# Second attention: two gathered rows per unit over 32 units in place of four over 16, and the first queries normalised ahead of the first gathers

## The chip, the core and the metric

The kernel runs on one core of a Trainium2 chip. The metric is the device time of one execution in microseconds, lower is better. The core has five engines with their own instruction queues, each worked off in order: PE (TensorE, matrix products), DVE (VectorE), ACT (ScalarE), POOL (GpSimd) and SP (SyncE, which only starts transfers here). They wait for one another through semaphores.

## What is computed

`x` is (8, 256, 256) in float32. Two blocks follow each other, and each does `x = x + attention(norm(x)) * silu(ffn(norm(x)))`. The change lies in the second block:

```
q, k, v = heads of xn @ wq.T, xn @ wk.T, xn @ wv.T     # 16 heads of 128
q = rope(rmsnorm(q, q_norm_w));  k = rope(rmsnorm(k, k_norm_w))
scores = 50 * tanh(q @ k.T * 128**-0.5 / 50), causal
s = softmax(scores) @ v @ wo.T
weights, indices = top_k(sigmoid(xn @ gate_w.T) + gate_b, 4)
g = shared_ffn(xn) + sum over the token's four experts of weight * expert(xn)
x = x + s * silu(g)
```

## The kernel before, in words

After the first block come the feed-forward part of the second block (a shared network, then 79 tiles of 128 routed rows), and then the second attention, from about 700 us to the end. The experts' results lie in DRAM, one row for each token and each of its four experts. They must be fetched back and added, weighted, to the gate sum `g1`. That is done beside the second attention.

The second attention is 64 units: 8 pairs of heads times 8 sequences of 256 tokens. A unit `n` goes through a pipeline that is three units deep, and each engine has the order of its work written out in a function `unit_pair(w, first)` of 16 units, run four times:

- PE in unit `n`: products for queries and keys in two halves (`project_qk`), transposes of the keys and of the normalised queries of unit `n-1` (`transposes_qk`), the product for the values (`project_v`), the mix with the values of `n-2` (`mix1`), the output product of `n-3` (`project_o`), the scores of `n-1` (`scores1`, lines 811 to 818; its first product, L817, marks the beat of a unit below), and the transposes of the mixed heads of `n-2` (`transposes_y`).
- ACT: copies `xs` (queries and keys) and `v` out of the accumulators, copies the transposed queries, takes tanh of the scores, rounds the transposed heads of `n-2` to `yT1h`, takes the exponential. In units 3 to 6 of every eight it also rounds a quarter of the next weights (`unit_hi`).
- DVE in unit `n`: squares and their sums in two halves (L1603, L1605), the mean squares (L1610), the scaled transposed keys `kT` of `n-1` (L1615), the division of the heads of `n-2`, the sum over heads of `n-3`, the low part `yT1l` of the heads of `n-2` (`out_lo`, L1212), and then, in the first 16 units, `combine(i)`: four operations (L1633), each adding one gathered row times its weight to `g1`, for the 128 tokens of tile `i`. In units 3 to 6 of every eight it ends with the low part of a quarter of the next weights (`unit_lo`, L1212, tile `bw_l`).
- POOL in unit `n`: `norm_q(n)` (a power, L1799, and two products, L1802), the causal mask of unit `n-1` (`mask`, L1811), and in the first 15 units `fetch_rows(i+1)`: four indirect gathers (L1827) of 128 rows each. Before unit 0 it waits until all rows of the experts are stored and issues `fetch_rows(0)`.

So tile `v` of 16 takes four gathers in one unit of POOL and four additions in one unit of DVE, one unit later than the gathers. `yg` has two buffers of four rows; a gather into a buffer waits until the tile before the last has been added (semaphore `g1_sb`). `gate_out1` (L1640) and `gate_tanh_out` turn `g1` into the gate in units 48 to 55.

Of the kernel before, what the change touches and what calls it, by code (L numbers as in the profile page):

```python
# [30 lines left out]
P = 128  # L31
NB, T, D = 8, 256, 256
TT, KD = T // P, D // P
NT = NB * TT
# [9 lines left out]
NE, TOPK, HE = 16, 4, 176  # L44
EW = KD * 2 * HE + 2 * D
NS = NT
CELLS = (NE + 1) * NT
NTILE = TOPK * NT + NE - 1
GROUP = 8
# [6 lines left out]
def build(nc, x, pack_qk, pack_vo, pack_w1, pack_w3, pack_w2, pack_attn, pack_experts, pack_shared, gate_b, q_norm, k_norm,  # L56
          rope_cosT, rope_sinT, ident_c, hadamard_c, tri_add_c, tri_mul_c, q_row_c, k_rows_c, before_c, route_c, out):
    ctx = ExitStack()
    with ctx:
        def sem(name):  # L60
            return ctx.enter_context(nc.semaphore(name))
# [22 lines left out]
        def region(start, end):  # L84
# [145 lines left out]
        y2_stored = [sem(f"y2_stored{j}") for j in range(GROUP)]  # L230
        xg_ps, up2_ps, z2_ps, down2_ps = (sem(n) for n in ("xg_ps", "up2_ps", "z2_ps", "down2_ps"))
        xT_sb, h2_sb, u2_sb, th2_sb, z2_sb, zT_sb, y2_sb, z2_clear = (sem(n) for n in (
            "xT_sb", "h2_sb", "u2_sb", "th2_sb", "z2_sb", "zT_sb", "y2_sb", "z2_clear"))
        yg_loaded = [sem("yg_loaded0"), sem("yg_loaded1")]
        g1_sb, thg_sb, gate_sb, so_sb, o_sb_made = (sem(n) for n in (
            "g1_sb", "thg_sb", "gate_sb", "so_sb", "o_sb_made"))

# [2 lines left out]
        def after(eng, s, value):  # L240

            if isinstance(value, int) and value <= 0:
                return
            eng.wait_ge(s, value)
# [956 lines left out]
        def _(dve):  # L1201
# [293 lines left out]
            def unit_lo(v, par, q):  # L1495
                half = (A_LOADS + par) % 2
                dve.wait_ge(bw_hi, 4 * v + q + 1)
                c = slice(512 * q, 512 * q + 512)
                lo(bw[par][1][:, c], raw[:, half, c], bw[par][0][:, c]).then_inc(bw_lo, 1)
# [100 lines left out]
            def squares(n, i, tt):  # L1600
                dve.wait_ge(xs_sb, 2 * n + tt + 1)
                x_qk = xs[:, i % 2, tt, :, :, :].rearrange("p s h e -> p (s h e)")
                dve.tensor_tensor(out=sq[:, tt, :], in0=x_qk, in1=x_qk, op=ALU.mult).then_inc(sq_sb, 1)  # L1603
                dve.wait_ge(sq_sb, 2 * n + tt + 1)
                dve.tensor_reduce(out=ssq[:, i % 2, tt, :], in_=sq[:, tt, :].rearrange("p (h e) -> p h e", h=4),  # L1605
                                  axis=AX.X, op=ALU.add).then_inc(ssq_sb, 1)

            def mean_squares(n, i):
                dve.wait_ge(ssq_sb, 2 * n + 2)
                dve.tensor_scalar(out=msq[:, i % 2, :], in0=ssq[:, i % 2, :, :].rearrange("p t h -> p (t h)"),  # L1610
                                  scalar1=1.0 / E1, scalar2=RMS_EPS, op0=ALU.mult, op1=ALU.add).then_inc(msq_sb, 1)

            def key_T(n, i, unit):
                dve.wait_ge(kT1_ps, n + 1)
                dve.tensor_tensor(out=kT1[:, i % 2, :, :], in0=more[:, 2, :].rearrange("p (h t) -> p h t", h=2),  # L1615
                                  in1=qk_scale[:, bass.ds(2 * unit, 2)].unsqueeze(2).to_broadcast([P, 2, T]),
                                  op=ALU.mult).then_inc(kT1_sb, 1)

            def heads_out1(n, i):
                dve.wait_ge(y1_ps, n + 1)  # L1620
                o = more[:, 0:2, 0:2 * (E1 + 1)].rearrange("p t (h e) -> p t h e", h=2)
                dve.reciprocal(out=rden1[:, i % 2, :, :], in_=o[:, :, :, E1]).then_inc(rden1_sb, 1)
                dve.wait_ge(rden1_sb, n + 1)
                dve.tensor_tensor(out=y1[:, i % 2, :, :, :], in0=o[:, :, :, 0:E1],
                                  in1=rden1[:, i % 2, :, :].unsqueeze(3).to_broadcast([P, TT, 2, E1]), op=ALU.mult)\
                   .then_inc(y1_sb, 1)

            def combine(v):

                dve.wait_ge(yg_loaded[v % 2], 16 * TOPK * (v // 2 + 1))  # L1630
                for k in range(TOPK):
                    after(dve, g1_sb, TOPK * v + k)
                    dve.scalar_tensor_tensor(out=g1[:, v, :], in0=yg[:, v % 2, k, :], scalar=prob_all[:, v, k:k + 1],  # L1633
                                             in1=g1[:, v, :], op0=ALU.mult, op1=ALU.add).then_inc(g1_sb, 1)

            def gate_out1(b):

                dve.wait_ge(thg_sb, b + 1)
                g = g1[:, TT * b:TT * b + TT, :].rearrange("p t d -> p (t d)")
                dve.scalar_tensor_tensor(out=g, in0=th_g[:], scalar=1.0, in1=g, op0=ALU.add, op1=ALU.mult)\  # L1640
                   .then_inc(gate_sb, 1)
# [11 lines left out]
            def add_unit(n, i, first, last=False):  # L1653
                b = i % NB
                dve.wait_ge(o1_ps, n + 1)
                s = s_acc[:, 2 * b:2 * b + 2, :].rearrange("p t d -> p (t d)")
                if first and 0 <= i < NB:
                    dve.tensor_copy(s, banks[1][:, :]).then_inc(acc1, 1)
                else:
                    after(dve, acc1, n + 1 - NB)  # L1660
                    dve.tensor_tensor(out=s, in0=banks[1][:, :], in1=s, op=ALU.add).then_inc(acc1, 1)
                if last:
                    block_out(b, s)

            def out_lo(n, i):
                dve.wait_ge(yT1h_sb, n + 1)
                lo(yT1l[:, i % 2, :, :].rearrange("p h t -> p (h t)"), trio[:, 2, :],
                   yT1h[:, i % 2, :, :].rearrange("p h t -> p (h t)")).then_inc(yT1l_sb, 1)

            def unit_pair(w, first, final):  # L1670
                for i in range(2 * NB):
                    n = 2 * NB * w + i

                    def live(lag):
                        return not first or i >= lag
                    squares(n, i, 0)
                    squares(n, i, 1)
                    mean_squares(n, i)
                    if live(1):
                        key_T(n - 1, i - 1, 2 * w + (i - 1) // NB)  # L1680
                    if live(2):
                        heads_out1(n - 2, i - 2)
                    if live(3):
                        add_unit(n - 3, i - 3, first, final and i - 3 >= NB)
                    if live(2):
                        out_lo(n - 2, i - 2)
                    if first:
                        combine(i)
                    if final and i < NB:
                        gate_out1(i)  # L1690
                    if 3 <= i % NB < 7 and not (final and i >= NB):
                        unit_lo(2 * w + i // NB + 1, (i // NB + 1) % 2, i % NB - 3)

            dve.wait_ge(rope_made, 6)
            unit_pair(0, True, False)
            for w in range(1, NU // 2 - 1):
                unit_pair(w, False, False)
            unit_pair(NU // 2 - 1, False, True)
            n = NU * NB
# [11 lines left out]
        def _(pool):  # L1711
# [84 lines left out]
            def norm_q(n, i):  # L1796
                r = i % 2
                pool.wait_ge(msq_sb, n + 1)
                pool.tensor_tensor(out=rstd[:, r, :], in0=msq[:, r, :], in1=half_pow[:], op=ALU.pow).then_inc(rstd_sb, 1)  # L1799
                pool.wait_ge(rstd_sb, n + 1)  # L1800
                for tt in range(TT):
                    last = pool.tensor_tensor(out=qn[:, r, tt, :, :], in0=xs[:, r, tt, 0, :, :],  # L1802
                                              in1=rstd[:, r, 4 * tt:4 * tt + 2].unsqueeze(2).to_broadcast([P, 2, E1]),
                                              op=ALU.mult)
                last.then_inc(qn_sb, 1)
# [8 lines left out]
            def unit_pair(w, first):  # L1814
                for i in range(2 * NB):
                    n = 2 * NB * w + i
                    norm_q(n, i)
                    if not first or i >= 1:
                        mask(n - 1, i - 1)
                    if first and i < NT - 1:  # L1820
                        fetch_rows(i + 1)

            def fetch_rows(v):

                after(pool, g1_sb, TOPK * (v - 1))
                for k in range(TOPK):
                    pool.indirect_dma_start(  # L1827
                        out=yg[:, v % 2, k, :], out_offset=None, in_=rows_dram,
                        in_offset=bass.IndirectOffsetOnAxis(ap=slots_all[:, v, k:k + 1], axis=0),
                        bounds_check=CELLS * P - 1, oob_is_err=False).then_inc(yg_loaded[v % 2], 16)  # L1830

            pool.wait_ge(down2_ps, NS + NTILE)
            pool.memset(v1[:].rearrange("p r t h e -> p (r t h) e")[:, :, E1:E1 + 1], 1.0).then_inc(v1_ones, 1)
            for j in range(GROUP):
                pool.wait_ge(y2_stored[j], 16 * ((NTILE - 1 - j) // GROUP + 1))
            fetch_rows(0)
            unit_pair(0, True)
            for w in range(1, NU // 2):
                unit_pair(w, False)
# [95 lines left out]
```

## Time and profile before

| | |
|---|---|
| median of 3 runs | 1366.03 us (1360.82 to 1368.21) |
| the profiled execution, own time | 1364.2 us |
| its span, first to last instruction | 1362.4 us |
| busy: PE, DVE, ACT, POOL | 1257.5, 847.7, 596.2, 472.7 us |
| mean granted PE clock | 0.975 of full speed |
| gathers (L1827) | 64, 68.7 us on POOL |
| additions (L1633) | 64, median 485 ns, longest 1391 ns |

Views are of this one execution. In a row of a timeline stand the start in us from the beginning of the span, the time in us, the engine, the source line, the operation, the tiles written and read, the shape, a count (x4 are four such instructions in a row), and in brackets the idle time of the engine before it with what ended it. Matrix products overlap, so a busy PE is a modelled one. The view by stretches gives for each window its length, the busy time of each engine with a count of instructions, the granted clock of PE (1.00 is 2.4 GHz) and the share and rate of transfers.

### The profile page before, as it was taken

The page shows a single profiled execution, that of the slowest core. Times are in us where ns is not written, and L with a number is a line of the kernel's source. Part 1 is how long each engine was busy: PE and PEld are TensorE (multiplying, and loading weights), DVE is VectorE, ACT ScalarE, POOL GpSimd, SP SyncE. Part 2 cuts the span into 40 slices and gives each one's busy share as a digit, 9 for nine tenths or more (in the row PEclk, how much of TensorE's full clock was granted, in tenths as well). Part 3 has the DMA queues.
Part 4 walks back from the last instruction along what each step waited for, and adds up shares of the span by engine and source line. Part 5 has one row for each costly group of instructions (what it writes and reads, how often), then busy time and mean ns, then how long its engine had stood idle before and what let it go on. Part 6 is the DMA issues. An engine that isn't in the chain of part 4 may idle for free.

```text
span 1362.4 us, 25374 instructions
## 1 busy us (share of the span) xinstructions
PE 1257.5 (92%) x9326; PEld 1095.7 (80%) x9326; DVE 847.7 (62%) x1733; ACT 596.2 (44%) x1351; POOL 472.7 (35%) x488
## 2 busy tenths in 40 slices
PE   5699989999988879999988899999999999999996
PEld 4588878778777757777767888899999999998995
DVE  4647567557556654434447777776666767676785
ACT  3333323323323335555544444445454545555552
POOL 0112332332431220000028787644434344434442
PEclk9799999989999989999999999999999999999998
DMA  5754224234100953333331221100000000000000
GB/s 203 280 194 152 104 103 151 78 129 148 47 33 27 346 188 105 105 103 103 109 121 53 67 65 47 63 1 32 1 1 32 1 32 1 1 1 1 1 32 32
DMA packets 63674, 112.20 MB, mean 82 GB/s; under 512 B 6977, under 2 KB 36033, under 8 KB 62017
## 3 DMA queue, kind: packets, MB, share of 16 engines
q1 hardware_dynamic: 57408, 93.79, 19.6%
q0 software_dynamic: 6144, 16.79, 3.7%
q8 instruction: 78, 1.28, 0.4%
q14 instruction: 44, 0.35, 0.1%
HBM read 49.86 MB, written 60.69 MB: 81 GB/s over the span
## 4 chain that ended last, share of the span: by engine, by line
PE 82%; DVE 8%; issue 4%; ACT 3%; another core or an unknown queue 2%; DMA 1%; POOL 0%; SPq 0%; ACTq 0%; DVEq 0%; POOLq 0%
PE bank L703 7%; PE six L720 6%; PE six L817 5%; PE bank L779 4%; PE bank L781 4%; PE bank L780 4%; PE bank L390 4%; PE bank L391 3%; PE bank L392 3%; PE bank L854 2%; PE bank L853 2%; PE bank L852 2%; PE bank L791 2%; PE six L831 2%; PE bank L792 2%
## 5 line engine op out<-in xcount | busy, mean ns | idle before, releaser
L1799 POOL TENSOR_TENSOR rstd<-msq,half_pow 128x8 f32<-128x8 f32 x64 | 105.4, 1647 | 156.6 <-DVE msq L1610 156.2
L1128 ACT ACTIVATE pT<-six,rstd 128x256 f32<-128x256 f32 x128 | 60.7, 475 | 215.3 <-PE six L818 212.9
L1736 POOL TENSOR_TENSOR hid_l<-hid,hid_h 128x256 fp32r<-128x256 f32 x64 | 48.0, 750 | 241.2 <-ACT hid_h L950 241.2
L1811 POOL TENSOR_TENSOR pT<-pT,tri_mul 128x512 f32<-128x512 f32 x64 | 84.3, 1316 | 129.1 <-ACT pT L1174 129.1
L1212 DVE TENSOR_TENSOR yT1l<-six,yT1h 128x512 fp32r<-128x512 f32 x64 | 44.3, 692 | 135.5 <-ACT yT1h L1179 135.5
L1603 DVE TENSOR_TENSOR sq<-xs 128x512 f32<-128x512 f32 x128 | 104.2, 814 | 17.2 <-ACT xs L1147 17.2
L703 PE MATMUL bank<-experts,xT 128*128 x316 | 109.5, 469 | 0.8 <-ACT xT L1072 0.8
L779 PE MATMUL bank<-bw_h,xT1h 128*128 128x512 f32 x256 | 106.2, 415 | 0.7 <-issue 0.7
L781 PE MATMUL bank<-bw_l,xT1h 128*128 128x512 f32 x256 | 100.5, 392 | 0.0
L780 PE MATMUL bank<-bw_h,xT1l 128*128 128x512 f32 x256 | 100.1, 391 | 0.0
L817 PE MATMUL six<-qT,kT 128*128 128x256 f32 x256 | 79.3, 392 | 19.0 <-issue 15.6
L1605 DVE TENSOR_REDUCE ssq<-sq 128x4 f32<-128x512 f32 x128 | 87.8, 686 | 4.4
L1152 ACT ACTIVATE v<-bank 128x512 f32<-128x512 f32 x64 | 38.3, 598 | 102.5 <-PE bank L793 102.5
L720 PE MATMUL six<-experts,zT 128*128 x316 | 81.5, 380 | 1.2 <-DVE zT L1552 1.2
L852 PE MATMUL bank<-bw_h,yT1h 128*128 128x256 f32 x256 | 77.4, 302 | 3.8 <-DVE yT1l L1212 3.8
L390 PE MATMUL bank<-xT0h,w_h 128*128 128x256 f32 x256 | 77.9, 304 | 2.7 <-DVE w_l L1212 2.5
L1802 POOL TENSOR_TENSOR qn<-xs,rstd 128x256 f32<-128x256 f32 x128 | 78.4, 632 | 5.1
L1147 ACT ACTIVATE xs<-bank 128x512 f32<-128x512 f32 x128 | 74.5, 618 | 8.2 <-PE bank L781 4.8
L791 PE MATMUL bank<-bw_h,xT1h 128*128 128x256 f32 x256 | 77.5, 303 | 0.5
L1552 DVE COPY zT<-six 128x256 f32<-128x256 f32 x95 | 40.3, 424 | 58.8 <-PE six L711 53.8
L929 ACT ACTIVATE pT<-six 128x768 f32<-128x768 f32 x64 | 48.4, 808 | 63.9 <-PE six L447 42.3
L1827 POOL DMA_INDIRECT yg<-cells_scratch,slots_all x64 | 68.7, 1074 | 20.1 <-issue 20.1
(282 smaller groups left out, 3926.7 us busy)
## 6 DMA issues: line engine op xcount, KB each, us to landing
cells_scratch<-zeros SPq DMA_DIRECT2D x8, 4352.0 KB, 14.8
xg<-cells_scratch SPq DMA_DIRECT2D x79, 128.0 KB, 2.0
cells_scratch<-y SPq DMA_DIRECT2D x79, 128.0 KB, 1.7
experts<-pack_experts_dram SPq DMA_DIRECT2D x16, 608.0 KB
raw<-pack_attn_dram SPq DMA_DIRECT2D x8, 1024.0 KB
raw<-pack_w_dram SPq DMA_DIRECT2D x2, 1024.0 KB
xT_scratch<-xT1h_c SPq DMA_DIRECT2D x8, 256.0 KB, 2.1
xT_scratch<-xT1l_c SPq DMA_DIRECT2D x8, 256.0 KB, 2.7
```

The lines of the kernel that those rows point to most:

```text
L390: pe.matmul(o, wh, mh, start=first, stop=False)
L703: last = pe.matmul(banks[j % 2][:, 0:2 * HE], xT[:, j % 2, k, :], weights(e, k * 2 * HE, 2 * HE), start=k == 0, stop=k == KD - 1)
L720: last = pe.matmul(six[:, 4 + r, 0:D], zT[:, r, c, :], w, start=c == 0, stop=c == 1)
L779: pe.matmul(banks[tt][:, :], xT1h[:, k, c], w[0][:, k, :], start=k == 0, stop=False)
L780: pe.matmul(banks[tt][:, :], xT1l[:, k, c], w[0][:, k, :], start=False, stop=False)
L781: last = pe.matmul(banks[tt][:, :], xT1h[:, k, c], w[1][:, k, :], start=False, stop=k == KD - 1)
L791: pe.matmul(o[:, tt, :], xT1h[:, k, c], w[0][:, k, :], start=k == 0, stop=False)
L817: pe.matmul(s_b[:, 0, h * T:(h + 1) * T], kT1[:, r, h, 0:P], qT1[:, r, h, :], start=True, stop=True)
L852: pe.matmul(o[:, tt, :], yT1h[:, r, h, c], w[0][:, h, :], start=h == 0, stop=False)
L1603: dve.tensor_tensor(out=sq[:, tt, :], in0=x_qk, in1=x_qk, op=ALU.mult).then_inc(sq_sb, 1)
L1605: dve.tensor_reduce(out=ssq[:, i % 2, tt, :], in_=sq[:, tt, :].rearrange("p (h e) -> p h e", h=4), axis=AX.X, op=ALU.add).then_inc(ssq_sb, 1)
L1799: pool.tensor_tensor(out=rstd[:, r, :], in0=msq[:, r, :], in1=half_pow[:], op=ALU.pow).then_inc(rstd_sb, 1)
```

## The change

Gathers and additions go by half tiles. `fetch_rows(u)` issues the gathers of two rows of tile `u // 2`, and `combine(u)` adds two. POOL issues `fetch_rows(n)` in unit `n` after the mask, for `n` from 0 to 31, and DVE runs `combine(n-1)` at its old place in the order of a unit, for `n` from 1 to 32. Four semaphores stand in for two. The wait for the stored rows of the experts, and the first gathers, come after `norm_q(0)` instead of before it, and DVE has no `combine` in unit 0 any more. The number of gathers and of additions stays 64 each.

```diff
-        yg_loaded = [sem("yg_loaded0"), sem("yg_loaded1")]
+        yg_loaded = [sem(f"yg_loaded{n}") for n in range(4)]
...
-            def combine(v):
-
-                dve.wait_ge(yg_loaded[v % 2], 16 * TOPK * (v // 2 + 1))
-                for k in range(TOPK):
+            def combine(u):
+
+                v, ks = u // 2, range(u % 2 * 2, u % 2 * 2 + 2)
+                dve.wait_ge(yg_loaded[u % 4], 32 * (u // 4 + 1))
+                for k in ks:
                     after(dve, g1_sb, TOPK * v + k)
                     dve.scalar_tensor_tensor(out=g1[:, v, :], in0=yg[:, v % 2, k, :], scalar=prob_all[:, v, k:k + 1],
                                              in1=g1[:, v, :], op0=ALU.mult, op1=ALU.add).then_inc(g1_sb, 1)
...
-                    if first:
-                        combine(i)
+                    if 1 <= n <= 2 * NT:
+                        combine(n - 1)
...
                     norm_q(n, i)
                     if not first or i >= 1:
                         mask(n - 1, i - 1)
-                    if first and i < NT - 1:
-                        fetch_rows(i + 1)
-
-            def fetch_rows(v):
-
+                    if n == 0:
+                        for j in range(GROUP):
+                            pool.wait_ge(y2_stored[j], 16 * ((NTILE - 1 - j) // GROUP + 1))
+                    if n < 2 * NT:
+                        fetch_rows(n)
+
+            def fetch_rows(u):
+
+                v = u // 2
                 after(pool, g1_sb, TOPK * (v - 1))
-                for k in range(TOPK):
+                for k in range(u % 2 * 2, u % 2 * 2 + 2):
                     pool.indirect_dma_start(
                         out=yg[:, v % 2, k, :], out_offset=None, in_=rows_dram,
                         in_offset=bass.IndirectOffsetOnAxis(ap=slots_all[:, v, k:k + 1], axis=0),
-                        bounds_check=CELLS * P - 1, oob_is_err=False).then_inc(yg_loaded[v % 2], 16)
+                        bounds_check=CELLS * P - 1, oob_is_err=False).then_inc(yg_loaded[u % 4], 16)
 
             pool.wait_ge(down2_ps, NS + NTILE)
             pool.memset(v1[:].rearrange("p r t h e -> p (r t h) e")[:, :, E1:E1 + 1], 1.0).then_inc(v1_ones, 1)
-            for j in range(GROUP):
-                pool.wait_ge(y2_stored[j], 16 * ((NTILE - 1 - j) // GROUP + 1))
-            fetch_rows(0)
             unit_pair(0, True)
```

## Rows read from the trace of the kernel before

**Rows 1.** Busy time by stretches: start of the attention, first 16 units, later units
```profile
700.60:720.00 19.40, 12.47 (x65) 10.47 (x64) 9.20 (x16) 4.46 (x8) 13.74 (x15) 0.94 0.49 172
...
840.00:870.00 30.00, 26.07 (x187) 23.93 (x186) 24.97 (x44) 13.47 (x28) 23.17 (x22) 1.00 0.22 66
...
940.00:980.00 40.00, 40.00 (x281) 37.08 (x280) 25.89 (x42) 21.09 (x47) 16.68 (x17) 1.00 0.08 28
```

**Rows 2.** Timeline of PE, first 16 units: the first score products of five units
```profile
738.50 0.67 PE L817 MATMUL six<-qT,kT 128*128 128x256 f32 x2 [0.86 <-issue]
...
771.95 0.67 PE L817 MATMUL six<-qT,kT 128*128 128x256 f32 x2 [1.31 <-issue]
...
783.10 0.67 PE L817 MATMUL six<-qT,kT 128*128 128x256 f32 x2 [1.32 <-issue]
...
793.65 0.67 PE L817 MATMUL six<-qT,kT 128*128 128x256 f32 x2 [0.72 <-issue]
...
880.43 0.67 PE L817 MATMUL six<-qT,kT 128*128 128x256 f32 x2 [0.73 <-issue]
```

**Rows 3.** Timeline of DVE, two of the first 16 units
```profile
778.87 0.69 DVE L1212 TENSOR_TENSOR bw_l<-raw,bw_h 128x512 fp32r<-128x512 f32 x1
...
786.56 0.69 DVE L1212 TENSOR_TENSOR yT1l<-six,yT1h 128x512 fp32r<-128x512 f32 x1 [2.15 <-ACT yT1h L1179]
787.17 2.94 DVE L1633 SCALAR_TENSOR_TENSOR g<-yg,prob_all,g 128x256 f32<-128x256 f32 x4
790.02 0.68 DVE L1603 TENSOR_TENSOR sq<-xs 128x512 f32<-128x512 f32 x1
...
792.86 0.68 DVE L1615 TENSOR_TENSOR kT<-six,qk_scale 128x512 f32<-128x512 f32 x1
```

**Rows 4.** Instructions of line L1633 in one unit, ns shortest/median/longest
```profile
L1633 DVE SCALAR_TENSOR_TENSOR g<-yg,prob_all,g x2: 486/934/1383, 787.7 to 789.1; 128x256 f32<-128x256 f32 x2
```

**Rows 5.** Timeline of POOL in the same unit: the mask and the first gather
```profile
787.34 1.45 POOL L1811 TENSOR_TENSOR pT<-pT,tri_mul 128x512 f32<-128x512 f32 x1 [1.33 <-ACT pT L1174]
788.94 1.09 POOL L1827 DMA_INDIRECT yg<-cells_scratch,slots_all  x1 [0.16 <-issue]
```

**Rows 6.** Timeline of PE, later units: the first score products of five units
```profile
890.11 0.59 PE L817 MATMUL six<-qT,kT 128*128 128x256 f32 x2
...
909.23 0.59 PE L817 MATMUL six<-qT,kT 128*128 128x256 f32 x2
...
1196.88 0.62 PE L817 MATMUL six<-qT,kT 128*128 128x256 f32 x2
...
1226.27 0.67 PE L817 MATMUL six<-qT,kT 128*128 128x256 f32 x2
...
1236.48 0.67 PE L817 MATMUL six<-qT,kT 128*128 128x256 f32 x2
```

**Rows 7.** Timeline of DVE in a later unit, which has no addition
```profile
904.27 1.38 DVE L1603 TENSOR_TENSOR sq<-xs 128x512 f32<-128x512 f32 x1 [0.53 <-ACT xs L1147]
...
907.80 0.68 DVE L1615 TENSOR_TENSOR kT<-six,qk_scale 128x512 f32<-128x512 f32 x1
```

**Rows 8.** Timeline of PE at the start of the attention
```profile
712.17 0.66 PE L808 MATMUL six<-ident,qn 128*128 128x128 f32 x4 [2.91 <-POOL qn L1802]
...
717.55 1.20 PE L817 MATMUL six<-qT,kT 128*128 128x256 f32 x2 [3.29 <-DVE kT L1615]
```

**Rows 9.** Timeline of DVE at the start of the attention
```profile
706.17 0.34 DVE L1610 TENSOR_SCALAR msq<-ssq 128x8 f32<-128x8 f32 x1
711.76 2.20 DVE L1633 SCALAR_TENSOR_TENSOR g<-yg,prob_all,g 128x256 f32<-128x256 f32 x4 [5.25 <-DMA yg<-cells_scratch,slots_all]
```

**Rows 10.** Timeline of POOL at the start of the attention
```profile
709.18 1.68 POOL L1799 TENSOR_TENSOR rstd<-msq,half_pow 128x8 f32<-128x8 f32 x1
```

**Rows 11.** Timeline of ACT at the start of the attention
```profile
714.79 0.59 ACT L1168 ACTIVATE qT<-six 128x512 f32<-128x512 f32 x1
```

**Rows 12.** Chain of waits at the start of the attention: start, us, what
```profile
708.15 3.58 DMA yg<-cells_scratch,slots_all
```

## Prediction

> **What bounds the kernel now.** I first looked at the page's forty slices. PE is busy nearly everywhere, but its digits fall to 8 in the five slices in which POOL's rise to 7 and 8: the first 16 of the 64 attention units. The view by stretches gives the size [rows 1]: in 30 us of the first 16 units PE is busy 26.07 us and POOL 23.17, in 40 us of later units PE is busy 40.00 of 40.00. POOL looks like the culprit, so I went to the timelines of the engines to see who waits for whom.
>
> The beat is the first score product of a unit on PE. In the first 16 units it comes at 771.95, 783.10 and 793.65, so 11.15 and 10.55 us apart, with PE idle 1.32 and 0.72 us just before it [rows 2]. From the third of these products at 738.50 to the sixteenth at 880.43 there are 13 intervals in 141.93 us: eight of 11.15 and five of 10.55 make 141.95. In the later units 32 intervals take 1196.88 - 890.11 = 306.77 us, 9.59 each [rows 6]. That is PE's own work, and the floor.
>
> What holds PE back is DVE's order. From the score product at 783.10: DVE finishes its `yT1l` (started 786.56) and starts the four additions at 787.17; the squares of the next unit start at 790.02, the keys at 792.86 (0.68 long), and at 793.65 PE multiplies with them [rows 2, 3]. The loop closes there, 10.55 us long. The unit before has `bw_l` between the additions and the squares (778.87), which makes the 11.15. The additions sit in this loop with 790.02 - 787.17 = 2.85 us. POOL is not in it: it stood idle 1.33 us before its mask [rows 5], waiting for ACT, which waited for the scores.
>
> The four additions aren't equal. The second is the long one, 1383 ns against 486 for the one after it [rows 4], and it lies beside the mask on POOL (787.34 to 788.79 [rows 5]). In a later unit, without additions, the same stall falls on the squares: 1.38 us instead of 0.68 [rows 7, 3]. So the stall of about 0.9 us belongs to the mask, and stays.
>
> **First 16 units: additions from four to two.** What goes is the third and the fourth, 2 x 0.486 = 0.97 us [rows 4]; counted from the end of the stalled one (787.68 + 1.38 = 789.06) to the squares at 790.02 it is 0.96, and DVE starts an independent operation up to 0.09 us before the last one ends. I take 1.0 us. Bounds: 0.96 from these rows, and 1.43 (half of the 2.85) if the stall shrank too. The eight intervals with `bw_l` then go from 11.15 to 10.15, still DVE's: 8 x 1.0 = 8.0 us. The five others would go to 9.55, just below PE's floor of 9.59: 5 x 0.96 = 4.8 us. Late next in these is PE itself.
>
> The Trainium skill (SBUF — State Buffer, "Who interferes with whom") says that a VectorE operation with two inputs in SBUF and a GpSimd operation that reads SBUF can't run together, and the later one waits for the whole of the other. The trace agrees with it in the 1383 ns; by this rule the stall stays and the price is two times 0.486, without it one would halve the whole block.
>
> **Units 16 to 31: two additions more.** In the loop of a later unit the keys start at 907.80, end at 908.48, and PE needs them at 909.23 [rows 6, 7]: 0.75 us of slack, and DVE was idle 0.53 us before the squares. Two additions of 0.97 fit, nearly to the hundredth (9.55 against 9.59), in the eight units without weights: cost 0, and 0.3 us in all at most if it misses by 0.04. With `bw_l` the loop is 10.15 against 9.59: 0.56 x 8 = 4.5 us lost. The trace has a precedent: 1226.27 to 1236.48 is 10.21 us [rows 6], a unit in which DVE has one other operation more (`gate_out1`) beside `bw_l`. With 10.21 the loss is 5.0, and the bound from above is that the eight others lose as much, 10.0 in all.
>
> **Gathers, two per unit over 32 units.** In the first 16 they take some 2.8 us off POOL, which bounds nothing there: worth 0 beyond the start. In units 16 to 31 they come after the mask. There POOL is busy 16.68 of 40 us, 4.0 in a unit of 9.59 [rows 1]; two gathers at about 1.4 from start to start (an estimate: the first of a group is 1.09 long [rows 5], and a gap follows) bring it to 6.8. The mask begins 4.24 us and ends 5.69 us after the score product [rows 2, 5], the gathers are issued by 8.5, and the next power waits for DVE's mean squares, which come just ahead of the keys, 8.8 us after the product with two additions (792.86 - 1.0 - 783.10). So they hide in POOL's wait for DVE. Without that cover each us beyond would delay the normalised queries by one, and PE's transposes wait for those.
>
> The new semaphores and the `g1_sb` wait of a gather add nothing: a buffer is reused four units later, after the additions of two units before.
>
> **The start.** DVE has the mean squares of unit 0 at 706.17 + 0.34 = 706.51 [rows 9], but POOL issues the first four gathers first and starts the power at 709.18 [rows 10]; PE waits 2.91 us for the queries until 712.17 [rows 8]. Then DVE, in `combine(0)`, waits 5.25 us for the gathers and adds until 713.96, and only then squares unit 1, so PE waits another 3.29 us for keys until 717.55 [rows 8, 9]. The stores that POOL waited for before the gathers are long done when `norm_q(0)` is, so moving it past them costs nothing; what now comes after it, two gathers, runs beside PE's value product, and the power of unit 1 follows them.
>
> After the change the queries are ready 709.18 - 706.51 = 2.67 us earlier, PE does the same transposes and value product, and ACT's copy of the transposed queries (714.79 + 0.59 = 715.38 [rows 11]) moves to 712.7. DVE loses the wait of 5.25 us, so the keys, ready at about 717.4 before, are ready by 712.2; their input is there, since PE made it before it stood still at 712.17 - 2.91 = 709.26. First score product: about 712.8 instead of 717.55, 4.75 us earlier. Bounds: 2.67 if only POOL's delay goes, 6.2 if both of PE's waits (2.91 + 3.29) go.
>
> The next two intervals, 717.55 to 738.50, take 20.95 us. The first product pair there lasts 1.20 us, later 0.67 [rows 8, 2], and the granted clock of the stretch is 0.94 [rows 1]: PE had stood still for 3.29 us and fell to 1.2 GHz. With at most 1.3 us of standing, as in the units of 11.15 whose clock is 1.00, it should not fall. I put 8.9 for the first (10.2 less 1.3) and 9.6 for the second: 2.4 us gained. Bounds: 1.0 (two additions once, the clock falls as before) and 3.8.
>
> **The sum.** 8.0 + 4.8 + 4.75 + 2.4 - 4.5 = 15.45 us. The profiled execution took 1364.2 us, so 1348.8; it lies 1.8 us under the median of 1366.03, from which the same sum gives 1350.6. I take 1350.
>
> **Rivals.**
>
> *A: the block halves.* If the stall shares in it, the loop loses 1.43 us: intervals of 9.72 and 9.59, gains of 8 x 1.43 + 4.8 = 16.2 and a loss of 8 x 0.13 = 1.0. Sum 22.4, 1342 to 1344. The same time would come out if POOL were the bound. For it: POOL's digits in the slices. Against it: POOL's idle 1.33 us [rows 5], and squares that stall without any addition [rows 7].
>
> *B: the second 16 units give more back, or the start gives less.* If all sixteen units there lose 0.62 (10.21 less 9.59), 10.0 us are paid, and the sum is 10; if instead the start gives only 2.67 + 1.0, it is 12. Both together 4.7. Time 1354 to 1361. For it: the slack in the units without weights is 0.04 us by my count.
>
> *C: the loop doesn't shorten,* because something that I don't see is late just behind DVE, and 16 more units get the longer one. Only the start remains, 1359 to 1366.
>
> *D, slower: DVE waits for rows that have not landed.* The last gather of a group took 3.58 us from issue to landing [rows 12], and DVE waited at the start [rows 9]. Now there are 32 such waits, in front of squares on which PE depends. The last of two gathers is issued 7.2 us after a score product (788.94 - 783.10, and 1.4 for the next) and needed 9.59 + 4.07 = 13.7 us after it: 6.4 us of slack. From a landing time of 6.4 us on, each unit pays the excess; the gain is used up when the excess is 15.4 / 32 = 0.5 us, and a landing of 7.3 us would give 1364 + 13 = 1377. Against it: no DVE wait for rows is seen inside the units above, with a slack of only about 4.5 us.
>
> **Chances.** My forecast 0.68, with its own range 1345 to 1355; A 0.08; B 0.15; C 0.06; D 0.03. I count 0.5%, 6.8 us, as what a measurement of this kernel can tell from no change. Faster by more than that: the forecast, A and most of B, 0.89. Within 0.5%: the rest of B and C, 0.08. Slower: D, 0.03. The range that should hold the time 8 times in 10 reaches over A's edge and half of B: 1342 to 1357.
>
> **What would show it.** The interval of score products: about 10.15 with `bw_l` and 9.6 without, in the first 16 units and in the next 16 alike; 9.59 from unit 33 on as before. One addition in two at about 1.38 us. The squares 1.0 us earlier after the score product than now. The first score product near 712.8, its pair 0.67 us long. POOL's power still ended by a wait for the mean squares in all units. I would be wrong in the place if units 16 to 31 stayed at 9.59 throughout, or if the units with weights fell to 9.7 (A); and wrong in the mechanism if the loop's PE idle stayed although DVE's keys come early (C), or if the additions show waits for DMA (D).

## The result and the profile after

The changed kernel takes 1347.41 us in the median of 4 runs (1344.74 to 1349.34), the one before 1367.12 in the median of 4 (1360.82 to 1369.58). The ratio is 0.9874, with a 95% interval from 0.9853 to 0.9896. I forecast 1350, 15.45 us less; it became 19.7 less by the medians. The profiled execution took 1344.74 us; its span, from the first to the last instruction, is 1343.0 in place of 1362.4.

Busy time by stretches of the changed kernel, which answers to [rows 1] (window, length, busy us of PE, PE's weight loads, DVE, ACT, POOL, then granted clock, share and rate of transfers):

```profile
700.60:720.00 19.40, 15.92 (x102) 13.87 (x101) 12.32 (x21) 7.50 (x15) 14.54 (x13) 1.00 0.33 123
840.00:870.00 30.00, 29.70 (x209) 27.41 (x209) 22.17 (x37) 15.39 (x34) 20.25 (x18) 1.00 0.19 63
940.00:980.00 40.00, 39.67 (x283) 36.81 (x283) 30.50 (x51) 20.59 (x44) 28.35 (x25) 1.00 0.09 28
```

PE is now busy 29.70 of 30 us in the first 16 units, where it was 26.07. The clock of the opening stretch is 1.00 and no longer 0.94. The third stretch shows the price: 39.67 of 40, and POOL at 28.35 where it had 16.68.

First score products of units on PE, answering to [rows 2, 6]:

```profile
758.54 0.67 PE L817 MATMUL six<-qT,kT 128*128 128x256 f32 x2 [0.28 <-issue]
...
768.65 0.67 PE L817 MATMUL six<-qT,kT 128*128 128x256 f32 x2 [0.32 <-issue]
...
778.31 0.59 PE L817 MATMUL six<-qT,kT 128*128 128x256 f32 x2
...
857.05 0.59 PE L817 MATMUL six<-qT,kT 128*128 128x256 f32 x2
...
905.91 0.67 PE L817 MATMUL six<-qT,kT 128*128 128x256 f32 x2 [0.27 <-issue]
...
916.02 0.67 PE L817 MATMUL six<-qT,kT 128*128 128x256 f32 x2 [0.29 <-issue]
...
1014.52 0.59 PE L817 MATMUL six<-qT,kT 128*128 128x256 f32 x2
```

The intervals with next weights are 10.11 us (768.65 - 758.54 in the first 16 units, 916.02 - 905.91 in the second), with PE idle about 0.3 us. Behind the last of four such units comes an interval of 9.66, in which PE doesn't wait.

DVE in one of the second 16 units, answering to [rows 3], and its two additions by duration, answering to [rows 4]:

```profile
909.37 0.69 DVE L1212 TENSOR_TENSOR yT1l<-six,yT1h 128x512 fp32r<-128x512 f32 x1 [2.15 <-ACT yT1h L1179]
909.98 1.90 DVE L1634 SCALAR_TENSOR_TENSOR g<-yg,prob_all,g 128x256 f32<-128x256 f32 x2
911.80 0.68 DVE L1212 TENSOR_TENSOR bw_l<-raw,bw_h 128x512 fp32r<-128x512 f32 x1
912.40 0.68 DVE L1603 TENSOR_TENSOR sq<-xs 128x512 f32<-128x512 f32 x1
...
915.23 0.68 DVE L1615 TENSOR_TENSOR kT<-six,qk_scale 128x512 f32<-128x512 f32 x1
```

```profile
L1634 DVE SCALAR_TENSOR_TENSOR g<-yg,prob_all,g x2: 477/931/1385, 910.0 to 910.5; 128x256 f32<-128x256 f32 x2
```

POOL in the same unit, answering to [rows 5]: the mask, the two gathers, and the power that still waits for DVE behind them.

```profile
910.15 1.44 POOL L1812 TENSOR_TENSOR pT<-pT,tri_mul 128x512 f32<-128x512 f32 x1 [1.91 <-ACT pT L1174]
911.75 1.09 POOL L1832 DMA_INDIRECT yg<-cells_scratch,slots_all  x1 [0.16 <-issue]
...
915.41 1.67 POOL L1800 TENSOR_TENSOR rstd<-msq,half_pow 128x8 f32<-128x8 f32 x1 [1.26 <-DVE msq L1610]
```

The start, all engines in order of time, answering to [rows 8 to 10]:

```profile
704.71 1.69 POOL L1803 TENSOR_TENSOR qn<-xs,rstd 128x256 f32<-128x256 f32 x2
...
706.45 0.66 PE L808 MATMUL six<-ident,qn 128*128 128x128 f32 x4 [0.66 <-POOL qn L1803]
...
709.76 0.67 PE L817 MATMUL six<-qT,kT 128*128 128x256 f32 x2 [1.22 <-ACT qT L1168]
...
711.12 1.58 DVE L1634 SCALAR_TENSOR_TENSOR g<-yg,prob_all,g 128x256 f32<-128x256 f32 x2 [2.65 <-DMA yg<-cells_scratch,slots_all]
```

PE's two waits are 0.66 and 1.22 us, where they were 2.91 and 3.29. The first additions still wait for rows, but the first score product is already out.

I cut both executions at the first product of the attention (700.59 before, 697.12 after) and at score products (us; a gain is positive; the end is known to 0.1 us only):

| part | before | after | gain | forecast |
|---|---|---|---|---|
| all ahead of the attention | 700.59 | 697.12 | 3.47 | 0 |
| to the first score product | 16.96 | 12.64 | 4.32 | 4.75 |
| next 2 intervals | 20.95 | 18.51 | 2.44 | 2.4 |
| 13 intervals of the first 16 units | 141.93 | 128.78 | 13.15 | 12.8 |
| 16 intervals after them | 153.47 | 157.47 | -4.00 | -4.5 |
| from there to the end | 328.50 | 328.48 | 0.02 | 0 |
| the attention | 661.81 | 645.88 | 15.93 | 15.45 |

Ahead of the attention PE's instructions are the same in both kernels. The difference there isn't one delay: by the starts of the same instructions it grows and shrinks, 1.7 us at 60 to 177 us, 0.4 at 202, 5.3 at 354 and 3.5 from 497 us on. The experiments have to say whether it belongs to the change.

### The profile page after: what moved, and what is told of

Read it like the earlier page. It is cut to its first block, busy times and chain, and to the rows that moved or that the text cites. A ratio compares the mean times of both kernels' runs of the same rounds, so it can differ in the third digit from the quotient of the medians.

```text
span 1343.0 us, 25390 instructions
## 1 busy us (share of the span) xinstructions
PE 1253.3 (93%) x9326; PEld 1093.4 (81%) x9326; DVE 847.5 (63%) x1733; ACT 596.6 (44%) x1351; POOL 482.5 (36%) x488
## 3 DMA queue, kind: packets, MB, share of 16 engines
q8 instruction: 78, 1.28, 0.4%
## 4 chain that ended last, share of the span: by engine, by line
PE 83%; DVE 8%; ACT 4%; issue 3%; another core or an unknown queue 2%; DMA 0%; POOL 0%; SPq 0%; ACTq 0%; DVEq 0%; POOLq 0%
PE bank L703 7%; PE six L720 6%; PE six L817 5%; PE bank L781 4%; PE bank L779 4%; PE bank L780 4%; PE bank L390 4%; PE bank L392 3%; PE bank L391 3%; PE bank L854 2%; PE bank L852 2%; PE bank L853 2%; PE bank L791 2%; PE bank L792 2%; PE bank L793 2%
## 5 line engine op out<-in xcount | busy, mean ns | idle before, releaser
L1812 POOL TENSOR_TENSOR pT<-pT,tri_mul 128x512 f32<-128x512 f32 x64 | 87.1, 1362 | 136.1 <-ACT pT L1174 136.1
L1603 DVE TENSOR_TENSOR sq<-xs 128x512 f32<-128x512 f32 x128 | 98.0, 765 | 14.3 <-ACT xs L1147 14.3
L1832 POOL DMA_INDIRECT yg<-cells_scratch,slots_all x64 | 74.9, 1170 | 15.0 <-issue 15.0
```

## The experiments

All ratios are against the kernel before on the same chip. Totals from different chips don't compare (before's median was 1336.79 us on the first, 1363.82 and 1365.84 on the two others), but the attention's length does: the changed kernel's, 645.88 us with a start at 697 us, came out as 646.2 in a second execution (start at 674) and as 646.1 in one without most of the gathers (start at 701). So I judge the steps by the attention and its parts.

One part is less even than the others. From unit 32's first score product to the end nothing but the edits to the gate and the mask shortens an interval. The other kernels took 327.5 to 329.0 us for it, and nearly all of that spread lies in the last two units. The interval between the last two of these products is 9.81 us in the kernel before, at a granted clock of 0.83, and 8.34 in the kernel with only the start changed, at 1.00. No edit bears on it. The time up to the 32nd of these products is therefore the sharper measure: 333.3 us before, 317.4 after.

**The changed kernel again.** No edit.

> The changed kernel once more, unchanged. Of the 19.4 us between the two profiled spans, 15.9 lie in the second attention and 3.5 before it, where both kernels hold the same instructions. If those 3.5 us are chance from one execution to the next, the median stands 15 to 17 us below before's in paired runs; if the change somehow speeds the code ahead of it, 19 to 20 us. Intervals of score products as in the first profile: 10.11 and 9.6 us.

Median 1321.89 us against 1336.79, ratio 0.9889 (0.9874 to 0.9904): 14.9 us less, 12.8 to 16.8 by the interval, so 19 to 20 is out. The attention took 646.21 us, its parts 12.64, 18.50, 128.72 and 157.50. The 3.47 us ahead of the attention are chance between executions: four kernels with the same instructions there reached it at 672.2 to 674.0 us on this chip, and two others at 701.5 and 706.2 on another. What the change gives is 15 to 16 us.

**Only the start.**

```diff
-                    if first:
-                        combine(i)
+                    if 1 <= n <= NT:
+                        combine(n - 1)
...
-                    if first and i < NT - 1:
-                        fetch_rows(i + 1)
+                    if n == 0:
+                        for j in range(GROUP):
+                            pool.wait_ge(y2_stored[j], 16 * ((NTILE - 1 - j) // GROUP + 1))
+                    if n < NT:
+                        fetch_rows(n)
```

> Only the start: four gathers and four additions per unit over 16 units as before, but the first gathers after the first queries' normalisation and the additions one unit later. Theory: the first score product comes 4.3 us earlier, the loop keeps 10.55 and 11.15 us, in all 4 to 6 us below before (1361 to 1363). Rival (the start gives the most, the loop was never DVE's): 10 us or more below before.

1334.58 us, ratio 0.9983 (0.9974 to 0.9992): 2.2 us less, a smaller gain than either expectation gave. The loop is as before: 13 intervals in 141.89 us. The first score product comes after 12.67 us, 4.3 earlier. But the next two intervals take 22.86 us in place of 20.95, and the additions, one unit later, lengthen a 17th unit, which costs 1.0. Up to the 32nd product 1.4 us are left. Its timeline, PE and DVE there:

```profile
684.88 0.67 PE L817 MATMUL six<-qT,kT 128*128 128x256 f32 x2 [1.22 <-ACT qT L1168]
...
688.86 3.48 DVE L1633 SCALAR_TENSOR_TENSOR g<-yg,prob_all,g 128x256 f32<-128x256 f32 x4 [5.29 <-DMA yg<-cells_scratch,slots_all]
...
696.04 0.98 PE L817 MATMUL six<-qT,kT 128*128 128x256 f32 x2 [2.44 <-DVE kT L1615]
```

With four gathers behind the first queries, DVE waits 5.29 us for them and then adds four rows, and PE waits 2.44 us for the keys of unit 1. Moving the gathers alone moves the wait by one unit; with two gathers it is 2.65 us and ends before PE needs the keys. The start's 4.3 us are kept only because the groups were halved.

**Only the spreading.**

```diff
-                    if 1 <= n <= 2 * NT:
-                        combine(n - 1)
+                    if n < 2 * NT:
+                        combine(n)
...
-                    if n < 2 * NT:
-                        fetch_rows(n)
+                    if n + 1 < 2 * NT:
+                        fetch_rows(n + 1)
...
+            for j in range(GROUP):
+                pool.wait_ge(y2_stored[j], 16 * ((NTILE - 1 - j) // GROUP + 1))
+            fetch_rows(0)
             unit_pair(0, True)
```

> Only the spreading: two gathers and two additions per unit over 32 units, but the first two gathers ahead of the first normalisation and the first additions in unit 0, as before. Theory: the loop gives 13.1 us back and the second 16 units cost 4.0, and since unit 0 now waits for two gathers and not four, the first score product still comes 3 to 4 us earlier: 12 to 14 us below before. Rival (only the start counted): 4 us below before or less.

1324.13 us, ratio 0.9907 (0.9892 to 0.9922): 12.7 us less, 11.8 up to the 32nd product. The loop gives the same as in the changed kernel (128.76 and 157.50 us). The split is other than I wrote: the first score product gains only 1.74 us (15.22), because DVE still waits for its two rows in unit 0, and the two intervals behind it gain 0.93 (20.02).

```profile
680.64 1.18 POOL L1803 TENSOR_TENSOR qn<-xs,rstd 128x256 f32<-128x256 f32 x2
...
681.87 0.66 PE L808 MATMUL six<-ident,qn 128*128 128x128 f32 x4 [0.33 <-POOL qn L1803]
...
683.50 1.00 DVE L1634 SCALAR_TENSOR_TENSOR g<-yg,prob_all,g 128x256 f32<-128x256 f32 x2 [4.71 <-DMA yg<-cells_scratch,slots_all]
...
688.09 1.19 PE L817 MATMUL six<-qT,kT 128*128 128x256 f32 x2 [4.13 <-DVE kT L1615]
```

After 4.13 us without work PE's first pair takes 1.19 us, against 0.67 after 1.22 us in the changed kernel: the granted clock from 686.6 to 693.4 us is 0.50, which is 1.2 GHz.

The run also says which half of the reordering pays. With two gathers ahead of the first normalisation PE has the queries 9.00 us after the start of the attention; with none, in the changed kernel, after 9.33 (11.58 before, with four). So the gathers' place on POOL is worth nothing to the queries once there are two. The 2.6 us between 15.22 and 12.64 come from the additions that left unit 0, where DVE waited 4.71 us for rows ahead of unit 1's squares, and PE 4.13 us for the keys behind them.

**Only the first eight gathers.**

```diff
-                    if n < 2 * NT:
+                    if n < 4:
                         fetch_rows(n)
...
-                dve.wait_ge(yg_loaded[u % 4], 32 * (u // 4 + 1))
+                dve.wait_ge(yg_loaded[u % 4], 32)
```

> The changed kernel with only the first 8 of the 64 gathers; later additions take what lies in the buffers (the fetching of the rows is left out, not the additions). Theory: POOL and the transfers are off the loop, so the intervals of score products stay at 10.11 and 9.6 us and the stall of the second addition at 1.38. Rival A in the form that POOL bounds the loop: the 10.11 falls to 9.6.

One execution, 1348.71 us. The attention takes 646.07 us with parts of 128.78 and 157.49: the same as with all gathers. DVE's additions don't change, and POOL just waits longer for DVE (3.81 us where it was 1.26):

```profile
L1634 DVE SCALAR_TENSOR_TENSOR g<-yg,prob_all,g x58: 474/928/1390, 746.1 to 1022.8; 128x256 f32<-128x256 f32 x58
```

```profile
761.64 1.64 POOL L1800 TENSOR_TENSOR rstd<-msq,half_pow 128x8 f32<-128x8 f32 x1 [3.81 <-DVE msq L1610]
```

Gathers at two per unit cost nothing in the loop of the changed kernel. That rules out D, and POOL as its bound. Of the kernel before, with four gathers per unit, the run says nothing; for that see the run with four in the gap.

**Half the mask.**

```diff
-                p = pT1[:, i % 2, :, :].rearrange("p h (c t) -> p h c t", c=3)[:, :, ::2, :]
-                pool.tensor_tensor(out=p, in0=p, in1=tri_mul[:].unsqueeze(1).unsqueeze(1).to_broadcast([P, 2, 2, P]),
+                p = pT1[:, i % 2, 0, :].rearrange("p (c t) -> p c t", c=3)[:, ::2, :]
+                pool.tensor_tensor(out=p, in0=p, in1=tri_mul[:].unsqueeze(1).to_broadcast([P, 2, P]),
                                    op=ALU.mult).then_inc(masked1, 1)
```

> The changed kernel with the causal mask on one of the two heads only (the other head is left unmasked), so that POOL's mask takes about 0.75 us in place of 1.45. Theory (the second addition stalls until the mask ends): it falls from 1.38 to about 0.7 us and the intervals with next weights from 10.11 to 9.6, PE's floor. Rival (the 1.38 us is the addition's own, from its weight or from waiting for the first addition's result): 1.38 and 10.11 stay.

One execution, 1337.60 us. The mask takes 0.90 us, not 0.75, and the longest addition 0.84, not 0.7; both moved down together, by 0.54:

```profile
753.92 0.90 POOL L1812 TENSOR_TENSOR pT<-pT,tri_mul 128x256 f32<-128x256 f32 x1 [1.91 <-ACT pT L1174]
```

```profile
753.75 1.35 DVE L1634 SCALAR_TENSOR_TENSOR g<-yg,prob_all,g 128x256 f32<-128x256 f32 x2
755.02 0.69 DVE L1212 TENSOR_TENSOR bw_l<-raw,bw_h 128x512 fp32r<-128x512 f32 x1
```

The intervals with weights fall to 9.57 and the attention to 635.75 us, 10.1 less, 9.3 of them up to the 32nd product. The 1.38 us of the second addition is the wait for the mask (its rival, the addition's own time, is out), and 0.54 us taken off one POOL operation is worth 0.54 us in each unit with next weights (at least, since 9.57 is PE's floor too). In units 51 to 54, which have the gate's operation beside the weights, the same edit brings only 0.15 (10.21 to 10.06). The mask is lengthened by the additions in turn, which I hadn't counted: in units without additions this half mask takes 0.73 us, and the whole mask takes 1.45 beside additions and 1.28 without.

**The additions in DVE's gap.** DVE waits 2.15 us for ACT ahead of `yT1l` in every unit. The additions go there, one unit later.

```diff
+                    if 2 <= n <= 2 * NT + 1:
+                        combine(n - 2)
                     if live(2):
                         out_lo(n - 2, i - 2)
-                    if 1 <= n <= 2 * NT:
-                        combine(n - 1)
```

> The changed kernel with the two additions moved ahead of the low part of the heads, into the 2.15 us in which DVE waits for ACT, and one unit later so that their rows have landed. Theory (the additions lie in the loop only because they stand behind yT1l): every interval with next weights falls from 10.11 to PE's 9.6, 16 x 0.5 = 8 us below the changed kernel. Rival C (something just behind DVE is late as well): 10.0 or so stays and nothing is gained. Rival D (waits for rows): DVE waits for DMA show up and the intervals grow.

1312.16 us against 1336.79, ratio 0.9817 (0.9804 to 0.9831). The attention takes 638.03 us, 7.9 less than in the changed kernel (8.0 up to the 32nd product, as expected): 13 intervals in 124.68 us and 16 in 153.57, 9.59 and 9.60 each, PE's floor. The timeline of DVE:

```profile
743.11 1.57 DVE L1634 SCALAR_TENSOR_TENSOR g<-yg,prob_all,g 128x256 f32<-128x256 f32 x2
745.34 0.69 DVE L1212 TENSOR_TENSOR yT1l<-six,yT1h 128x512 fp32r<-128x512 f32 x1 [0.67 <-ACT yT1h L1179]
746.56 1.39 DVE L1603 TENSOR_TENSOR sq<-xs 128x512 f32<-128x512 f32 x1 [0.53 <-ACT xs L1147]
```

The additions take longer there in sum (1.57 us) than two of 0.49, and it doesn't matter. The mask's stall is back on the squares, as in [rows 7]. The additions were in the loop only through their place.

**The same without the unit of delay.**

```diff
-                    if 2 <= n <= 2 * NT + 1:
-                        combine(n - 2)
+                    if 1 <= n <= 2 * NT:
+                        combine(n - 1)
```

> The additions ahead of the low part of the heads, but without the unit more of delay: the rows are wanted about 2.8 us earlier than in the changed kernel. The last of two gathers is issued 7.2 us after a score product and lands 3.6 us later, at 10.8; DVE gets there at 9.6 + 1.3 = 10.9. Theory: at most short waits, hidden by the gap, and the time of the kernel with the delay (within 1 us). Rival D (rows land late enough to matter): waits of 1 us or more in each of 32 units, intervals over 10 us, 10 us or more above the kernel with the delay.

1338.39 us against 1363.82, ratio 0.9824 (0.9795 to 0.9853); attention 637.23 us, parts of 124.77 and 153.50, and up to the 32nd product the same 309.4 us as with the delay. There are waits for rows now, six in all:

```profile
L1634 DVE SCALAR_TENSOR_TENSOR g<-yg,prob_all,g x64: 483/718/815, 712.1 to 1008.8; 128x256 f32<-128x256 f32 x64
its engine sat idle before it (us, times) until:
  DMA yg<-cells_scratch,slots_all: 7.9, 6
```

The first, 2.73 us, is the start's. Of the others four come eight units apart, 0.97 to 1.44 us long. They fit the landing times of the kernel with the delay, where a gather takes 3.2 us from issue to landing in the median, but the two of these very units take 5.7 and 4.5. The gap swallows the waits, so even with 2.8 us less to land in, D's landing time doesn't reach the loop. The slack is smaller than the median suggests, though.

**Four in the gap, over 16 units.** The edit is to the kernel with only the start changed.

```diff
+                    if 2 <= n <= NT + 1:
+                        combine(n - 2)
                     if live(2):
                         out_lo(n - 2, i - 2)
-                    if 1 <= n <= NT:
-                        combine(n - 1)
```

> Four gathers and four additions per unit over 16 units, as before, but first gathers after the first normalisation, and the additions in DVE's gap one unit later. It asks whether spreading was needed at all once the additions are off the loop. Theory: the additions (1.97 us) fit into the 2.15 us gap, so DVE leaves the loop, and POOL becomes the bound: power 1.68, products 1.3, mask 1.6 and four gathers 5.4 us make 10.0 us, so intervals near 10.0 in the first 16 units, with and without next weights, and 9.6 after; 3 to 6 us above the kernel with two per unit in the gap. Rival (POOL never binds): 9.6 everywhere, the same time as with two per unit.

1352.94 us against 1365.84, ratio 0.9906 (0.9884 to 0.9928); attention 649.47 us, 11.4 above two per unit in the gap (11.1 up to the 32nd product). I had expected 3 to 6. The 13 intervals take 133.03 us, 10.23 each and not 10.0, which is 8.4 above two per unit; the two intervals before them are 1.8 longer, and a 17th unit with additions costs 0.9. POOL's timeline has no wait left but pauses of 0.3 us or less, and PE waits for POOL's queries:

```profile
798.22 1.70 POOL L1799 TENSOR_TENSOR rstd<-msq,half_pow 128x8 f32<-128x8 f32 x1
800.00 1.19 POOL L1802 TENSOR_TENSOR qn<-xs,rstd 128x256 f32<-128x256 f32 x2
801.14 1.74 POOL L1811 TENSOR_TENSOR pT<-pT,tri_mul 128x512 f32<-128x512 f32 x1
803.04 1.35 POOL L1830 DMA_INDIRECT yg<-cells_scratch,slots_all  x1 [0.16 <-issue]
...
808.34 1.68 POOL L1799 TENSOR_TENSOR rstd<-msq,half_pow 128x8 f32<-128x8 f32 x1
...
811.78 0.66 PE L808 MATMUL six<-ident,qn 128*128 128x128 f32 x4 [0.76 <-POOL qn L1802]
```

From power to power it is 10.12 us of POOL's own work. POOL was the second bound, just behind DVE, hidden until DVE was out of the way. Spreading the gathers is needed after all, for POOL's sake.

**The gate in the gap.** On top of the additions in the gap with the delay: `gate_out1(i - 1)` also ahead of `out_lo`.

```diff
+                    if final and 1 <= i <= NB:
+                        gate_out1(i - 1)
                     if live(2):
                         out_lo(n - 2, i - 2)
-                    if final and i < NB:
-                        gate_out1(i)
```

> The kernel with the additions in DVE's gap, and the gate's operation of units 48 to 55 moved into the same gap one unit later. Theory: the four last long intervals fall from 10.22 to 9.6, 2.4 us below the kernel with the additions in the gap, 27 below before. Rival: there ACT's extra tanh ahead of the copies makes the 10.22, and nothing is gained.

1338.57 us against 1363.82, ratio 0.9826 (0.98 to 0.9851). The four intervals (units 51 to 54) fall from about 10.2 only to 9.96, 1.0 us in all: neither the theory nor the rival.

**The gate's tanh earlier as well.** ACT's `gate_tanh_out` goes ahead of the tanh of the scores, with two buffers for `th_g`.

```diff
-        th_g = sbb("th_g", [P, TT * D])
+        th_g = sbb("th_g", [P, 2, TT * D])
...
                     key_query(n - 1, i - 1)
+                    if final and i < NB:
+                        gate_tanh_out(i)
                     scores_exp(n - 1, i - 1)
...
-                if final and i < NB:
-                    gate_tanh_out(i)
```

> The kernel with the additions and the gate's operation in DVE's gap, and now ACT's gate tanh ahead of the scores' tanh, where ACT waits 3 us, with two buffers for it. Theory: the 9.96 us that were left in units 51 to 54 came from ACT, whose gate tanh (0.66 us) stood ahead of the copies that PE's value product waits for; they fall to 9.6, 1.4 us below the kernel before it. Rival: DVE's order is still the limit there and 9.96 stays.

1340.44 us against 1365.84, ratio 0.982 (0.9798 to 0.9842). The four intervals are 9.55, 9.66, 9.61 and 9.61 now, 1.4 us less than without this edit: the rest was ACT's. PE at two of these score products:

```profile
1216.88 0.61 PE L817 MATMUL six<-qT,kT 128*128 128x256 f32 x2
...
1226.49 0.62 PE L817 MATMUL six<-qT,kT 128*128 128x256 f32 x2
```

The attention lasts 635.58 us, 10.3 less than in the changed kernel, and every interval from the third on lies between 9.55 and 9.66. The total stands 25.4 us below before. By totals the four versions with the additions in the gap (ratios 0.9817 to 0.9826) can't be told apart; by the intervals this last one is the best.

## Why the prediction was right

**The loop.** I had it as score product, `yT1l`, additions, squares, keys, score product, on DVE, with POOL outside. For the changed kernel this is shown from both sides: removing nearly all gathers changed nothing (646.07 us), and moving the additions freed the loop (638.03). Rival A's second form, POOL as the bound, is out for the kernel before, though only by little: the same four gathers and four additions per unit, with the additions off DVE's loop, run at 10.23 us, where the kernel before held 10.55 and 11.15.

One sign was read wrongly. I wrote that POOL's power would "still" be ended by a wait for the mean squares. In the first 16 units before the change it wasn't: it started straight behind the last gather, without a wait and 0.6 to 1.3 us after the mean squares were ready:

```profile
783.05 1.69 POOL L1799 TENSOR_TENSOR rstd<-msq,half_pow 128x8 f32<-128x8 f32 x1
```

That did no harm only because POOL then had its 1.33 us of idle time ahead of the mask. With two gathers the power does wait, 1.26 us in the units with weights and 0.14 in the others.

**The price of two additions.** I took 1.0 us off the intervals with weights, for 10.15; they became 10.11 (10.04 for the first of each four). A's first form, half of the 2.85 us, would have given 9.72. The reason for the difference, the stall that belongs to the mask, is shown by the half mask: mask and stalled addition shrink together by 0.54 us. The stalled addition ends 0.28 us after the mask in both runs, a little less than the 0.49 it takes alone, so it waits for nearly the whole of the mask and not quite all. The 13 intervals gave 13.15 for my 12.8.

**The second 16 units.** I charged 0.56 us for each of eight units and nothing for the others; they paid 4.00 us for my 4.5. B, ten us paid there, is out, and so is its other half, a start worth 3.67 us (it gave 6.76 with the two intervals behind it). C is out as well. B's sum was wrong besides: both halves together leave 6.5 us of the 15.45 and not 4.7, so its slow end was 1359.5 and not 1361. The stated range doesn't depend on it.

**The start.** 4.32 us for my 4.75. The step that was off is the time at which the queries are ready: I moved POOL's power and products by 2.67 us as they were, but the two products took 1.69 us in place of 1.18. Before, behind the power of [rows 10], they were

```profile
710.94 1.18 POOL L1802 TENSOR_TENSOR qn<-xs,rstd 128x256 f32<-128x256 f32 x2
```

They now lie beside DVE's squares of unit 1 (one of which took 0.92 us instead of 0.68); in the run with only the spreading, where no squares lie beside them, they took 1.18 again. So PE got the queries only 2.25 us earlier. The clock step held: the first pair took 0.67 us, the stretch shows 1.00, and the two intervals gave 2.44 for my 2.4. What I had not seen is how much the start depends on the spreading: alone, with four rows, it is worth 1.4 us up to the 32nd product. The attention's 659.49 us against 661.81 say 2.3, but 1.0 of that is the uneven end.

**D.** Waits for rows occurred once, 2.65 us at the start and off PE's path.

**The size.** By the steps the forecast was 0.5 us off, and that is in part luck: I had the loop's gain 0.35 us too small and the price of the second 16 units 0.5 too large, and the start's gain 0.4 too large. The medians' 19.7 us hold some 4 us that the steps don't; the repeat gave 14.9.

## What to carry to other kernels

Find the loop that closes a pipelined unit before counting busy time: an operation costs what it adds to that loop, and the same operation a few places earlier in its queue, in a wait of that engine, cost nothing here. Look for the second bound too; here it stood 0.3 to 0.9 us behind the first, and it decided whether spreading the gathers was needed. When a long duration in a group is a stall, find out whose it is, since removing neighbours doesn't remove it.

## What the runs showed of the hardware

- A DVE operation with both inputs in SBUF issued while POOL's mask ran took 1.38 to 1.39 us (addition or squares, alone 0.49 and 0.68). The addition ended 0.28 us after the mask, the squares 0.55. With a mask of 0.90 us the addition took 0.84 and still ended 0.28 after it. I had read this in the trace before; that it goes the other way as well I had not counted: the mask took 1.45 us beside the additions and 1.28 without them, POOL's products took 1.69 us beside DVE's squares in the start, and its mask up to 1.74 us in the kernel with four gathers per unit and the additions in the gap.
- PE's first pair of products took 1.20 and 1.19 us after 3.29 and 4.13 us without work, 0.98 after 2.44, and 0.67 after 1.22. The granted clock behind the first three was 0.53 (717.4 to 721 us, before), 0.50 (686.6 to 693.4, only the spreading) and 0.51 (696.2 to 699.7, only the start). One wait of such a length isn't always followed by the low clock: the kernel before also waited 2.91 us for the first queries, and its clock was 1.00 from 700.6 to 717.4.
- The part ahead of the attention, with the same instructions, took 672 to 674 us in four executions on one chip and 697 to 706 in eight on others, while the attention of two kernels that differ only in gathers agreed within 0.2 us. The end of the attention isn't as steady: the last two units and what follows them took 37.3 to 38.8 us, with the granted clock of one interval at 0.83 or 1.00. A step of this size is read better from its own stretch than from totals.
- A gather of 128 rows landed 3.2 us after its issue in the median of the kernel with the additions in the gap (2.7 to 5.7); the slow ones came once in eight units.
